# A first pass that puts four image rows on a partition and its filter taps on quarters of the array

## The chip, the core and the metric

The kernel runs on one core of one Trainium2 chip. The metric is the time of one execution in microseconds (us) of the device. Five engines work beside each other, each through its own list of instructions: TensorE (PE; its weight loads are a row of their own, PEld), VectorE (DVE), ScalarE (ACT), GpSimd (POOL) and SyncE (SP, which issues the transfers here). They meet at semaphores only. The transfers themselves are done by 16 DMA engines.

## The reference, cut to what matters

Two layers over x of shape 8 x 512 x 128 x 128, float32. The first layer halves the image by a grouped 3 x 3 convolution (two input channels make one of 256 output channels), finds clusters and a gate from that small image, and adds its gated, enlarged copy to x:

```
x1 = conv(x, w_down, strides (2, 2), padding 1, groups 256)     # 8 x 256 x 64 x 64
...                                                             # k-means, mixture, gate from x1
up = repeat(gate * x1 + x1, 2, axis=1) * w_up
x  = bilinear_up_x2(up) + x
```

The second layer projects that x on 8 x 8 cosine patterns over the image and uses the 64 numbers of each channel for an attention:

```
P  = einsum('hu,wv->hwuv', Dh, Dv)      # 16384 x 64
xP = einsum('bcn,nk->bck', x, P)
...                                     # attention from xP; gamma * out + x
```

Since the projection is linear, the kernel takes it of the raw x and of x1 apart.

## The kernel before, in words

The kernel has a first pass over all of x (268 MB), a short stretch that finds clusters and gates from what the pass left, and a second pass that reads x again and writes the output. The change is in `first_pass` and in the constants that it reads, and nowhere else.

**Tiles.** A unit is two input channels, that is one output channel, of all 8 images: 1 MB in `xt`, one of 14 buffers. A partition holds two adjacent rows (r = 0, 1) of one channel, so 2 channels x 64 pairs of rows fill the 128 partitions, and a piece of a load is 1 KB. Four units are a group; there are 64 groups.

**Tap products.** For each unit POOL builds `band`, three columns of 64 x 64 weights on 128 rows (lines 206 and 213). PE (`convolve`, line 278) makes the convolution of a pair of units in one PSUM bank: unit e = 0 on the left column half of the array and e = 1 on the right one, six taps each (two rows r, three column shifts dw), all 128 rows of the array. ACT copies the bank to `staged` (line 260), SP stores it to `xd` in DRAM (line 155) in pieces of 256 bytes, one row of 64 numbers of one image.

**Projection.** `project` (line 294) multiplies the group's x by the 8 cosines over the rows: 16 matmuls of 32 columns on four column quarters. DVE multiplies by the cosines over the columns and sums (lines 225 and 229). Every fourth group `project_low` (line 307) does the same with `staged`.

**What sets the order.** Each engine's list is written out. PE: the two pairs of a group, in every fourth group the small projection, then the group's projection. SP: the group's two stores (each waits for ACT's copy), then the loads of four units, which wait until the projection has freed their buffers; halfway and at the end eight stores of `freq` (`store_freq`, line 164). All transfers share SP's one queue and land in about the order of issue. POOL builds bands up to eight units ahead.

## Time and profile before

| | |
|---|---|
| median of 3 runs | 2952.55 us (2927.55 to 2962.68) |
| profiled execution | 2949.2 us, span 2947.4 us |
| first pass | to about 1007 us of the span |
| PE busy in the whole span | 2531.7 us (86%) |
| DVE, ACT, POOL busy | 2141.5, 1185.5, 1040.4 us |
| read and written in DRAM | 615.0 and 303.6 MB |

A row of the trace gives an engine, the line of the kernel that issued, the tiles (out<-in, buffer numbers left out) and times. Busy times of PE are unions of records whose ends are modelled, so the starts of its records tell more than their lengths. A matmul of the program leaves two records here. The share of the DMA engines is the sum of their packets' times over 16 engines, and can pass 1 where packets overlap. What an engine waited for is inferred from semaphores.

### The profile page before, as it was taken

How to read it: one execution, taken by the hardware profiler on the slowest of the kernel's cores; microseconds unless marked ns; L12 is line 12 of the kernel's file. 1: busy time of each engine (PE TensorE's matmuls, PEld its weight loads, DVE VectorE, ACT ScalarE, POOL GpSimd, SP SyncE). 2: the span in 40 equal slices, each digit the busy share in tenths (PEclk: the TensorE clock that was granted, in tenths of full speed). 3: DMA queues.
4: the chain of work that ended last, by engine and by line, in shares of the span. 5: the costliest groups of instructions: out<-in, count | busy, mean ns of one | idle time of the engine just before them, and what ended most of it. 6: DMA issues, size and time to landing. Idle time of an engine off the chain costs nothing.

```text
span 2947.4 us, 46132 instructions
## 1 busy us (share of the span) xinstructions
PE 2531.7 (86%) x17638; PEld 1666.6 (57%) x17638; DVE 2141.5 (73%) x2317; ACT 1185.5 (40%) x3193; POOL 1040.4 (35%) x772
## 2 busy tenths in 40 slices
PE   8999999999999666378499989888888887888887
PEld 2233223233323164044389888878778887788776
DVE  3777767677766743165499998988788888888886
ACT  0000000000000020033377777767666676766764
POOL 5444444444444000000044444444434343343433
PEclk9999999999999875689699999999999999999998
DMA  9999999999999660630499999999999999999998
GB/s 318 305 313 307 298 303 316 298 300 309 309 298 304 193 281 18 187 38 0 177 357 416 416 415 402 406 390 380 384 370 386 371 389 374 385 361 376 375 379 326
DMA packets 622924, 923.48 MB, mean 313 GB/s; under 512 B 208641, under 2 KB 471169, under 8 KB 620290
## 3 DMA queue, kind: packets, MB, share of 16 engines
q1 hardware_dynamic: 622722, 920.73, 90.1%
q8 instruction: 134, 2.20, 0.3%
q14 instruction: 68, 0.56, 0.0%
HBM read 615.00 MB, written 303.56 MB: 312 GB/s over the span
## 4 chain that ended last, share of the span: by engine, by line
DMA 33%; PE 11%; DVE 3%; ACT 2%; issue 2%; SPq 1%; POOL 0%; DVEq 0%
DMA out<-second_x 25%; PE second_o L1245 7%; DMA second_x<-in_x 4%; DMA second_dd<-downsampled 4%; DVE second_x L1469 1%; PE second_mid_t L1215 1%; DVE second_left L1018 1%; DVE second_mid L1450 1%; SPq L1051 1%; PE second_st L1105 1%; ACT second_mid L1334 1%; ACT second_left L1346 1%; POOL second_left L1018 0%; PE second_zt_t L1228 0%; ACT second_part L1334 0%
## 5 line engine op out<-in xcount | busy, mean ns | idle before, releaser
L1245 PE MATMUL second_o<-second_right,second_left 128*128 128x128 f32 x8192 | 1081.4, 281 | 110.9 <-issue 44.3
L1018 POOL TENSOR_TENSOR second_left<-second_mid_copy,second_coef_rep 64x1024 f32<-64x1024 f32 x256 | 608.6, 2377 | 1350.5 <-ACT second_mid_copy L1355 1329.5
L1245 PEld LDWEIGHTS second_o<-second_right,second_left 128*128 128x128 f32 x8192 | 999.3, 196 | 144.8 <-issue 134.7
L1469 DVE SCALAR_TENSOR_TENSOR second_x<-second_o,second_shift,second_x 128x512 f32<-128x512 f32 x1024 | 735.3, 738 | 222.9 <-PE second_o L1245 118.3
L278 PE MATMUL first_conv<-first_x,first_band 128*64 128x512 f32 (+1 forms) x3072 | 735.6, 618 | 19.4 <-POOL first_band L213 11.2
L278 PEld LDWEIGHTS first_conv<-first_x,first_band 128*64 128x64 f32 x3072 | 238.3, 135 | 510.5 <-issue 460.5
L225 DVE TENSOR_TENSOR first_product<-first_freq,first_cols 128x4096 f32<-128x4096 f32 x64 | 283.2, 4424 | 310.5 <-PE first_freq L294 310.0
L206 POOL TENSOR_TENSOR first_band<-first_shift,first_w_all 128x576 f32<-128x576 f32 x256 | 289.6, 1152 | 541.1 <-PE first_conv L278 533.8
L260 ACT ACTIVATE first_staged<-first_conv 128x512 f32<-128x512 f32 x128 | 76.5, 597 | 923.5 <-PE first_conv L278 923.5
L1334 ACT ACTIVATE second_mid<-second_dd,all_inter 128x128 f32<-128x128 f32 x1024 | 313.3, 388 | 85.8 <-DMA second_dd<-downsampled 83.6
L1334 ACT ACTIVATE second_part<-second_dd,all_inter 128x128 f32<-128x128 f32 x1024 | 313.2, 388 | 3.2
L1018 DVE TENSOR_TENSOR second_left<-second_mid_t,second_coef_rep 64x1024 f32<-64x1024 f32 x256 | 308.3, 1204 | 0.9 <-PE second_mid_t L1215 0.6
L229 DVE TENSOR_REDUCE first_freq<-first_product 128x32 f32<-128x4096 f32 x64 | 282.9, 4420 | 2.2
L1215 PE MATMUL second_mid_t<-all_const,second_mid 128*128 128x128 f32 x1024 | 166.3, 287 | 98.1 <-DVE second_mid L1450 97.4
L1355 ACT ACTIVATE second_mid_copy<-second_mid_t 64x512 f32<-64x512 f32 x256 | 151.6, 592 | 213.6 <-PE second_mid_t L1215 210.5
L294 PE MATMUL first_freq<-first_x,first_rows 128*32 128x512 f32 x2048 | 232.6, 594 | 0.0
L1215 PEld LDWEIGHTS second_mid_t<-all_const,second_mid 128*128 128x128 f32 x1024 | 118.2, 145 | 117.9 <-DVE second_mid L1450 113.9
L1450 DVE TENSOR_TENSOR second_mid<-second_mid,second_part 128x1024 f32<-128x1024 f32 x128 | 162.5, 1269 | 3.5 <-ACT second_part L1334 3.5
L294 PEld LDWEIGHTS first_freq<-first_x,first_rows 128*32 128x32 f32 x2048 | 61.5, 110 | 165.7 <-issue 165.7
L213 POOL TENSOR_TENSOR first_band<-first_band 128x192 f32<-128x192 f32 x256 | 147.4, 597 | 0.0
L1358 ACT ACTIVATE second_right<-second_zt_t 64x256 f32<-64x256 f32 x256 | 96.7, 378 | 122.0 <-PE second_zt_t L1228 120.5
L1228 PE MATMUL second_zt_t<-all_const,second_zt 128*128 128x128 f32 x512 | 101.8, 282 | 0.0
(219 smaller groups left out, 1415.9 us busy)
## 6 DMA issues: line engine op xcount, KB each, us to landing
first_x<-in_x SPq DMA_DIRECT2D x256, 1024.0 KB, 11.0
second_x<-in_x SPq DMA_DIRECT2D x256, 1024.0 KB, 14.3
out<-second_x SPq DMA_DIRECT2D x256, 1024.0 KB, 16.4
downsampled<-first_staged SPq DMA_DIRECT2D x128, 256.0 KB, 8.6
gather_d<-downsampled SPq DMA_DIRECT2D x16, 2048.0 KB, 16.4
second_dd<-downsampled SPq DMA_DIRECT2D x64, 512.0 KB, 14.9
second_p<-in_p_cols SPq DMA_DIRECT2D x1, 4096.0 KB
gates_ft<-all_wv SPq DMA_DIRECT2D x64, 32.0 KB, 5.4
```

The lines of the kernel that those rows point to most:

```text
L206: nc.gpsimd.tensor_tensor(band[unit % WEIGHTS1][:, :, :, :], shift[:, :, :].unsqueeze(2).broadcast_to([P, 3, 3, HD]), w_all[:, unit, :].re ...
L225: nc.vector.tensor_tensor(product[:, :, :, :], freq_ps[g % FREQ_BANKS][:, :, :].unsqueeze(2).broadcast_to(shape), cols[:, :, :].unsqueeze( ...
L229: nc.vector.tensor_reduce(freq[:, g, :, :], product[:, :, :, :], AX.X, ALU.add).then_inc(freq_summed, 1)
L278: last = nc.tensor.matmul(bank[e * HD:(e + 1) * HD, :, left:], band[unit % WEIGHTS1][:, 1 + r, dw + 1, :], xt[unit % SLOTS1][:, :, r, at:a ...
L294: last = nc.tensor.matmul(bank[32 * q:32 * q + 32, :, :], rows[:, r, j, :], xt[unit % SLOTS1][:, half * HALF_B:(half + 1) * HALF_B, r, :], ...
L1018: return eng.tensor_tensor(left[a][rows, odd:HALF:2, :, :].rearrange("p n (t s) g -> p n t s g", t=T), turned[rows, :, :, :].unsqueeze(3). ...
L1215: last = nc.tensor.transpose(mid_t[:, n, t, :], mid[m % 2][:, t, r:r + 2, :].rearrange("p h w -> p (h w)"), k("ident"))
L1245: last = nc.tensor.matmul(ob[n][:, r, :], left[a][:, r, n, :], right[a][:, r, :], start=True, stop=True)
L1334: last = nc.scalar.activation((mid[c], part)[r][:, :, 2 * i + 1 - e, :], dd[:, :, row(i + e + r - 1), :], ACT.Copy, scale=row_w[:, 2 * e + ...
L1355: nc.scalar.activation(mid_copy[hi, :, :, :], mid_t[hi, :, :, :], ACT.Copy).then_inc(mid_copied, 1)
L1450: nc.vector.tensor_tensor(mid[c][:, :, :, :], mid[c][:, :, :, :], part[:, :, :, :], ALU.add).then_inc(interpolated, 1)
L1469: nc.vector.scalar_tensor_tensor(out=xt[i][:, n // S, n % S, rows, :], in0=ob[n][:, :, :], scalar=shift[:, n:n + 1], in1=xt[i][:, n // S, ...
```

## The change

A tile is now four input channels (two output channels) with four adjacent rows of an image on a partition: 4 channels x 32 blocks of rows on the 128 partitions, 2 MB, loaded in pieces of 2 KB; seven buffers in place of fourteen, two tiles a group. A channel pair lies on one half of the partitions, so a tap product uses 64 rows of the array: k picks the row half (and the PSUM bank), a the tile and the column half. Rows r = 1 and r = 3 of a block serve an even and an odd output row each, so their products are 64 columns wide; r = 0 and r = 2 serve one, 32 wide. Even output rows stand on partitions 0 to 31 of a half, odd ones on 32 to 63; so a bank is stored by four transfers of 32 partitions in place of one. The bands come ready from one multiplication, as `shift` and the weights are laid out for it on the host.

```
-SLOTS1 = 14
-WEIGHTS1 = 8
+BLOCK1 = 4
+BLOCKS1 = H // BLOCK1
+TILES1 = GROUPS1 * 2
+SLOTS1 = 7
+WEIGHTS1 = 4
+EDGES = [(1, (2, 0)), (3, (0, 2)), (0, (1,)), (2, (1,))]
+BANDS = [dh for _r, dhs in EDGES for dh in dhs]
...
-    xv = x.rearrange("b (c s) (i r) w -> c (s i) b (r w)", s=S, r=2)
-    xdv = xd.rearrange("b t g (h w) -> (t g h) b w", w=WD)
+    xv = x.rearrange("b (n q) (i r) w -> n (q i) b (r w)", q=2 * S, r=BLOCK1)
+    xdv = xd.rearrange("b t g (i e w) -> (t g) e i b w", e=2, w=WD)
...
-        xt = [sc.sb(f"x{i}", [P, B, 2, W]) for i in range(SLOTS1)]
+        xt = [sc.sb(f"x{i}", [P, B, BLOCK1, W]) for i in range(SLOTS1)]
...
-                    if unit >= SLOTS1:
-                        sp.wait_ge(freq_made, (unit - SLOTS1) // GROUP1 + 1)
+                    if tile >= SLOTS1:
+                        sp.wait_ge(freq_made, (tile - SLOTS1) // 2 + 1)
...
                     sp.wait_ge(conv_copied, pair + 1)
-                    sp.dma_start(xdv[pair * P:(pair + 1) * P], staged[pair % STAGED][:, :, :]
-                                 ).then_inc(stored[pair % STAGED], 16)
+                    for a in range(2):
+                        for e in range(2):
+                            at = a * 64 + e * 32
+                            sp.dma_start(xdv[pair // 2 * GROUP1 + 2 * a + pair % 2, e], staged[pair % STAGED][at:at + 32, :, :]
+                                         ).then_inc(stored[pair % STAGED], 16)
...
                     for pair in (2 * g, 2 * g + 1):
                         store(pair)
-                    for unit in range(g * GROUP1 + SLOTS1, (g + 1) * GROUP1 + SLOTS1):
-                        if unit < UNITS1:
-                            load(unit)
+                    for tile in range(2 * g + SLOTS1, 2 * g + 2 + SLOTS1):
+                        if tile < TILES1:
+                            load(tile)
...
-                    for unit in units:
-                        b = band[unit % WEIGHTS1]
-                        pool.wait_ge(scaled, unit + 1)
-                        nc.gpsimd.tensor_tensor(b[:, 2, :, :], b[:, 2, :, :], b[:, 0, :, :], ALU.add).then_inc(banded, 1)
+                for tile in range(TILES1):
+                    if tile >= WEIGHTS1:
+                        pool.wait_ge(conv_made, (tile - WEIGHTS1) // 2 + 1)
+                    nc.gpsimd.tensor_tensor(
+                        band[tile % WEIGHTS1][:, :, :, :], shift[:, :, :].unsqueeze(1).broadcast_to(shape),
+                        w_all[:, tile, :].rearrange("p (a b) -> p a b", a=3).unsqueeze(3).broadcast_to(shape),
+                        ALU.mult).then_inc(banded, 1)
...
+                def convolve(g):
+
+                    if g >= CONV_BANKS // 2:
+                        pe.wait_ge(conv_copied, 2 * (g - CONV_BANKS // 2) + 2)
+                    pe.wait_ge(banded, 2 * g + 2)
+                    for tile in (2 * g, 2 * g + 1):
+                        pe.wait_ge(x_in[tile % SLOTS1], (tile // SLOTS1 + 1) * 16)
+
+                    def product(r, n, width, place, dw, first, last):
                         left = 1 if dw < 0 else 0
                         at = dw + 2 * left
+                        for a in range(2):
+                            for k in range(2):
+                                tile, part = 2 * g + a, slice(k * 64, k * 64 + 64)
+                                made = nc.tensor.matmul(
+                                    conv_ps[(2 * g + k) % CONV_BANKS][a * HD + place:a * HD + place + width * BLOCKS1,
+                                                                      :, left:],
+                                    band[tile % WEIGHTS1][part, dw + 1, n:n + width, :].rearrange("p n i -> p (n i)"),
+                                    xt[tile % SLOTS1][part, :, r, at:at + 2 * (WD - left) - 1:2],
+                                    start=first, stop=last)
+                        return made
+
+                    for dw in (0, 1, -1):
+                        product(1, 0, 2, 0, dw, dw == 0, False)
+                        product(3, 2, 2, 0, dw, False, False)
+                    for dw in (0, 1, -1):
+                        product(0, 4, 1, 0, dw, False, dw < 0)
+                        made = product(2, 5, 1, BLOCKS1, dw, False, dw < 0)
+                    made.then_inc(conv_made, 1)
...
-                    for n in range(4):
-                        j, r = n // 2, n % 2
+                    for r in range(BLOCK1):
                         for q in range(4):
-                            half, up = q // 2, q % 2
-                            unit = g * GROUP1 + 2 * up + j
-                            last = nc.tensor.matmul(bank[32 * q:32 * q + 32, :, :], rows[:, r, j, :],
-                                                    xt[unit % SLOTS1][:, half * HALF_B:(half + 1) * HALF_B, r, :],
-                                                    start=n == 0, stop=n == 3)
+                            half, a = q // 2, q % 2
+                            last = nc.tensor.matmul(
+                                bank[32 * q:32 * q + 32, :, :], rows[:, r, :],
+                                xt[(2 * g + a) % SLOTS1][:, half * HALF_B:(half + 1) * HALF_B, r, :],
+                                start=r == 0, stop=r == BLOCK1 - 1)
```

On SP, from the start of the program through the first groups, the list before was this (line, kind, out<-in, shape, how many in a row; L149 are the loads, L155 the stores):

```order
L174 DMA first_shift<-in_first_cols 128x192
L174 DMA first_rows<-in_first_cols 128x128
L174 DMA first_low_rows<-in_first_cols 128x64
L175 DMA first_w_all<-in_w_rows 128x2304
L149 DMA first_x<-in_x 128x8x256 x2
L180 DMA first_cols<-in_first_cols 128x1024
L180 DMA first_low_cols<-in_first_cols 128x512
L149 DMA first_x<-in_x 128x8x256 x12
L155 DMA downsampled<-first_staged 128x8x64 x2
L149 DMA first_x<-in_x 128x8x256 x4
L155 DMA downsampled<-first_staged 128x8x64 x2
L149 DMA first_x<-in_x 128x8x256 x4
```

With the change the same stretch has half as many loads of twice the size, and eight stores where two stood (L154 loads, L163 stores):

```order
L154 DMA first_x<-in_x 128x8x512 x2
L188 DMA first_cols<-in_first_cols 128x1024
L188 DMA first_low_cols<-in_first_cols 128x512
L154 DMA first_x<-in_x 128x8x512 x5
L163 DMA downsampled<-first_staged 32x8x64 x8
L154 DMA first_x<-in_x 128x8x512 x2
L163 DMA downsampled<-first_staged 32x8x64 x8
L154 DMA first_x<-in_x 128x8x512 x2
```

Stores still stand ahead of the loads of their group, in one block. On PE, the first group and the start of the second were this before (the shape is that of the result, columns of the array by elements):

```order
L278 MATMUL first_conv<-first_x,first_band 64x512 x8
L278 MATMUL first_conv<-first_x,first_band 64x8x63 x4
L278 MATMUL first_conv<-first_x,first_band 64x512 x8
L278 MATMUL first_conv<-first_x,first_band 64x8x63 x4
L294 MATMUL first_freq<-first_x,first_rows 32x512 x16
L278 MATMUL first_conv<-first_x,first_band 64x512 x8
```

And with the change (L282 the tap products, L306 the projection):

```order
L282 MATMUL first_conv<-first_x,first_band 64x512 x16
L282 MATMUL first_conv<-first_x,first_band 64x8x63 x8
L282 MATMUL first_conv<-first_x,first_band 32x512 x16
L282 MATMUL first_conv<-first_x,first_band 32x8x63 x8
L306 MATMUL first_freq<-first_x,first_rows 32x512 x16
L282 MATMUL first_conv<-first_x,first_band 64x512 x16
```

There are 48 tap products a group where 24 stood, 24 of them 64 columns wide and 24 of them 32, each on 64 rows of the array; the projection keeps its 16.

## Rows read from the trace of the kernel before

**Rows 1.** Busy by stretch, first pass: PE, PEld, DVE, ACT, POOL, PEclk, DMA share, GB/s
```profile
0.00:1007.00 1007.00, 987.18 (x5376) 306.61 (x5376) 691.89 (x157) 77.76 (x129) 431.76 (x516) 1.00 1.01 303
```

**Rows 2.** Costliest groups on the page, PE and POOL of the first pass
```profile
L278 PE MATMUL first_conv<-first_x,first_band 128*64 128x512 f32 (+1 forms) x3072 | 735.6, 618 | 19.4 <-POOL first_band L213 11.2
...
L206 POOL TENSOR_TENSOR first_band<-first_shift,first_w_all 128x576 f32<-128x576 f32 x256 | 289.6, 1152 | 541.1 <-PE first_conv L278 533.8
...
L294 PE MATMUL first_freq<-first_x,first_rows 128*32 128x512 f32 x2048 | 232.6, 594 | 0.0
...
L213 POOL TENSOR_TENSOR first_band<-first_band 128x192 f32<-128x192 f32 x256 | 147.4, 597 | 0.0
```

**Rows 3.** PE in order of time, 88 to 165 us: start, length, line
```profile
101.84 3.64 PE L294 MATMUL first_freq<-first_x,first_rows 128*32 128x512 f32 x32
105.41 11.03 PE L278 MATMUL first_conv<-first_x,first_band 128*64 128x512 f32 x48
116.37 3.64 PE L294 MATMUL first_freq<-first_x,first_rows 128*32 128x512 f32 x32
...
130.89 3.64 PE L294 MATMUL first_freq<-first_x,first_rows 128*32 128x512 f32 x32
...
147.16 3.62 PE L294 MATMUL first_freq<-first_x,first_rows 128*32 128x512 f32 x32
```

**Rows 4.** Weight loads in order of time, 405 to 413 us
```profile
407.03 0.14 PEld L278 LDWEIGHTS first_conv<-first_x,first_band 128*64 128x64 f32 x2 [0.31 <-issue]
407.48 0.14 PEld L278 LDWEIGHTS first_conv<-first_x,first_band 128*64 128x64 f32 x2 [0.30 <-issue]
...
409.81 0.13 PEld L294 LDWEIGHTS first_freq<-first_x,first_rows 128*32 128x32 f32 x4 [0.30 <-issue]
410.24 0.13 PEld L294 LDWEIGHTS first_freq<-first_x,first_rows 128*32 128x32 f32 x4 [0.30 <-issue]
```

**Rows 5.** Waits to 1100 us, PE's for loads: us in total, times, longest
```profile
PEld first_conv L278 <- DMA first_x<-in_x: 26.8, 30, 2.8
...
PE first_conv L278 <- DMA first_x<-in_x: 8.0, 10, 1.8
```

**Rows 6.** Waits of SP's queue, to 1007 us
```profile
SPq L155 <- ACT first_staged L260: 70.8, 50, 4.2
SPq L149 <- PE first_freq L294: 67.3, 51, 3.1
```

**Rows 7.** Line 294 alone: durations, first and last start
```profile
L294 PE MATMUL first_freq<-first_x,first_rows x2048: 592/592/617, 27.5 to 1004.3; 128*32 128x512 f32 x187
```

**Rows 8.** SP in order of time, 300 to 350 us: start, length, line
```profile
306.12 5.81 SPq L155 DMA_DIRECT2D downsampled<-first_staged  x2
311.97 9.64 SPq L149 DMA_DIRECT2D first_x<-in_x  x4
321.65 6.25 SPq L155 DMA_DIRECT2D downsampled<-first_staged  x2
```

**Rows 9.** Busy by stretch, as rows 1: store stretch, next loads, second pass
```profile
312.00:318.00 6.00, 6.00 (x42) 1.48 (x38) 0.00 (x0) 0.60 (x1) 3.36 (x4) 1.00 0.82 202
318.00:327.00 9.00, 8.81 (x40) 2.66 (x38) 8.81 (x2) 0.60 (x1) 3.27 (x4) 1.00 1.09 353
...
1600.00:1700.00 100.00, 92.55 (x763) 85.50 (x761) 92.00 (x121) 76.78 (x215) 44.62 (x19) 1.00 1.03 416
```

**Rows 10.** DMA packets, stretches 16–44 (loads), 1425.5–1428 (2 KB loads), 996.5–999 us (stores)
```profile
DMA packets 9654, 9.75 MB, mean 348 GB/s; under 512 B 144, under 2 KB 9653, under 8 KB 9653
...
DMA packets 520, 1.00 MB, mean 400 GB/s; under 512 B 32, under 2 KB 32, under 8 KB 520
...
DMA packets 2181, 0.55 MB, mean 220 GB/s; under 512 B 2181, under 2 KB 2181, under 8 KB 2181
```

**Rows 11.** Issues: loads on the page, to landing; SP in time, 1010–1020 us
```profile
first_x<-in_x SPq DMA_DIRECT2D x256, 1024.0 KB, 11.0
...
1013.89 4.13 SPq L164 DMA_DIRECT2D projected<-first_freq  x8
```

More of the change, by code:

```diff
@@ L175, in _ @@
                 sp.dma_start(w_all[:, :, :].rearrange("p c k -> p (c k)"), w_rows).then_inc(const_in, 16)
-                for unit in range(SLOTS1):
-                    load(unit)
-                    if unit == 1:
+                for tile in range(SLOTS1):
+                    load(tile)
+                    if tile == 1:
                         for n in (3, 4):
@@ L184, in _ @@
                         store(pair)
-                    for unit in range(g * GROUP1 + SLOTS1, (g + 1) * GROUP1 + SLOTS1):
-                        if unit < UNITS1:
-                            load(unit)
+                    for tile in range(2 * g + SLOTS1, 2 * g + 2 + SLOTS1):
+                        if tile < TILES1:
+                            load(tile)
                     if g == GROUPS1 // 2:
@@ L193, in _ @@
                 for i in range(STAGED):
-                    sp.wait_ge(stored[i], len(range(i, pairs, STAGED)) * 16)
+                    sp.wait_ge(stored[i], len(range(i, pairs, STAGED)) * 64)
                 sp.wait_ge(freq_out, 2 * 2 * GROUP1 * 16)
@@ L272, in convolve @@
                         left = 1 if dw < 0 else 0
                         at = dw + 2 * left
-                        for e in range(2):
-                            unit = 2 * pair + e
-                            if n == 0:
-                                pe.wait_ge(x_in[unit % SLOTS1], (unit // SLOTS1 + 1) * 16)
-                            last = nc.tensor.matmul(bank[e * HD:(e + 1) * HD, :, left:],
-                                                    band[unit % WEIGHTS1][:, 1 + r, dw + 1, :],
-                                                    xt[unit % SLOTS1][:, :, r, at:at + 2 * (WD - left) - 1:2],
-                                                    start=n == 0, stop=n == len(TAPS) - 1)
@@ L282, in convolve @@
-                    last.then_inc(conv_made, 1)
+                        for a in range(2):
[7 more added lines that the diff above has]
+                                    start=first, stop=last)
@@ L1598, in shape_constants @@
     side, high, low = row // UV, row // LOW % LOW, row % LOW
-    own, at = row // HD, row % HD
-    halo = np.stack([at[:, None] + 1 == np.arange(HD)[None, :]] + [at[:, None] == np.arange(HD)[None, :]] * 2, 1)
-    turned = np.stack([[d[2 * at + r][:, None, :] * (2 * j + own[:, None, None] == np.arange(4)[None, :, None])
-                        for j in range(2)] for r in range(2)]).transpose(2, 0, 1, 3, 4)
-    low_turned = np.stack([du[at][:, None, :] * (2 * j + own[:, None, None] == np.arange(4)[None, :, None])
+    own, at = row // BLOCKS1, row % BLOCKS1
+    here_, next_ = at[:, None] == np.arange(BLOCKS1)[None, :], at[:, None] + 1 == np.arange(BLOCKS1)[None, :]
+    halo = np.stack([next_ if n == 2 else here_ for n in range(len(BANDS))], 1)
+    turned = np.stack([d[BLOCK1 * at + r][:, None, :] * (own[:, None, None] == np.arange(4)[None, :, None])
+                       for r in range(BLOCK1)], 1)
+    half, h_low = row // HD, 2 * (row % BLOCKS1) + row // BLOCKS1 % 2
+    low_turned = np.stack([du[h_low][:, None, :] * (j + 2 * half[:, None, None] == np.arange(4)[None, :, None])
                            for j in range(2)], 1)
```

46 lines of the change are left out of this document (16 added, 30 removed).

## The prediction

> **What bounds the kernel now.** I first read the busy table by stretch [rows 1]: the first pass, to 1007 us, keeps PE busy 987 us of 1007 and the DMA engines at 1.01, while DVE has 692, POOL 432 and ACT 78. The change touches this stretch alone, so two candidates are left. The costliest groups [rows 2] say what PE does in it: 3072 records of L278 (the tap products), 2048 of L294 (the projection), two records for each matmul of the program. A busy PE is no proof of a bound, so the second view is the order of time on PE where nothing waits [rows 3]. From one projection to the next it is 14.53 us (101.84 to 116.37), and 16.27 us in every fourth group, which has L307 too (130.89 to 147.16). Over four groups that is 59.86 us, 14.97 each: the pace PE would keep if never held. The weight loads give the step [rows 4]: tap products start every 0.45 us, two records at a time (column halves); projections every 0.43 us, four at a time (column quarters). So 24 steps of 0.45 = 10.80 of the 10.96 us from 105.41 to 116.37, and 8 of 0.43 = 3.44 of the 3.57 us after it; 0.16 and 0.13 us go at the changes of tile shape.
>
> The real pace is slower. L294 starts from 27.5 to 1004.3 us [rows 7]; less the last projection's seven steps that is 63 groups in 973.8 us, 15.46 each. The 0.49 us between this and 14.97, times 64, is 31 us, and the waits list has it: 26.8 + 8.0 us for first_x [rows 5]. SP waits 71 + 67 us in all [rows 6], and over whole groups it sits inside one issue after the other [rows 8]. **PE and DMA are both near their limit, DMA slightly nearer.** A gain needs both.
>
> What DMA does with a group of 4.19 MB of loads and 0.52 MB of stores is in the stretches. Loads alone, 1 KB packets, run at 348 GB/s [rows 10], so they take 12.05 us. The stores' stretch (312 to 318 us) moves only 202 GB/s at a share of 0.82, and the next is back at 353 [rows 9]. In those 6 us 1.21 MB moved, 0.69 MB of it loads, worth 1.97 us at 350; the group's stores took the other 4.03 us. Stores alone run at 220 GB/s [rows 10], 2.38 us a group. The rest is lost in the turn from stores to loads. On the mean over the pass, 15.46 − 12.05 = 3.41 us is what a group's stores cost.
>
> **The change, part by part.**
>
> *Loads.* 256 loads of 1 MB in 1 KB pieces become 128 of 2 MB in 2 KB pieces, the same bytes. The trace has 2 KB loads by themselves for 2.5 us: 400 GB/s [rows 10]. So 10.49 us a group, 1.56 less. The bounds are 348 (no gain) and the 416 GB/s of 4 KB packets later in the run [rows 9]; I take 400, the same packet size, though from a short stretch.
>
> *Stores.* The same 256-byte pieces, but eight issues of 64 KB a group in place of two of 256 KB. The nearest rows are the eight 64 KB stores of L164, taken up in 4.13 us, 0.52 each [rows 11]. SP then needs 8 × 0.52 + 2 × 0.5 = 5.2 us a group, well inside 14. The turn to loads stays once a group, since the eight follow each other. I keep 3.41 us; ends 2.38 (turn hidden) and 4.03. The new stride in DRAM (every second row) I cost at nothing, as each piece was separate already; the upper end holds it otherwise.
>
> *Tap products.* Per group 48 matmuls in place of 24, each on half the rows. The 64-wide ones (24, rows r = 1 and 3) fill four quarters of the array, the 32-wide ones (24, r = 0 and 2) come as two products on different column quarters, so eight fit. If what fits runs together, that is 12 + 6 = 18 steps of 0.45 where 24 stood, 2.70 us less, and one more change of shape, 0.15 more: 14.53 becomes 11.98, the mean over four 12.4. No row shows row halves, so I bound it: steps as short as now, or one half after the other. I take the first because the projection's four streams [rows 4] show the array taking unlike operands at once without a longer step; eight records per step at the spacing of those is still no burden.
>
> *POOL.* 256 second steps (L213, 147 us) and one of two waits go; 128 builds of 576 elements stay at 1.15 us [rows 2]. POOL was hidden behind PE, so nothing is gained: its 2.3 us a group are covered by the two groups that it builds ahead. DVE's order is unchanged, 692 / 64 = 10.8 us a group, under any period here. ACT's two copies (78 / 128 = 0.6 us each) now follow each other; ACT has little else to do.
>
> *Lead and ends.* Seven 2 MB buffers hold what fourteen did. After project(g) SP loads the second tile of group g+3 and the first of g+4, and PE needs g+3 two groups later, 28 us, against 11.0 to land now [rows 11]. PE's start now wants 4 MB in place of 2, some 6 us later, which a pass bound by loads doesn't feel.
>
> **The sum.** A group is 10.49 + 3.41 = 13.90 us, above PE's 12.4. The last load follows the stores of 61 groups: 64 × 10.49 + 61 × 3.41 = 879 us, behind some 6 us of constants (2.2 MB by their shapes, at 350), so 885. Then PE does the last taps and seven steps of projection, 8.4 + 3.0: its last start is at 896 against 1004.3, **108 us earlier**. All behind it is unchanged work on unchanged data. Against the profiled execution (2949.2 us, span 2947.4; the median of the runs is 2952.6, 0.1% above) that gives 2841; I add 6 us for PE holding the queue in some groups, its 12.4 being near: **2847 us**. With stores at 2.38 it would be about 2780, at 4.03 some 2880; loads at 380 instead of 400 add 35.
>
> **A rule against it.** The eight 64 KB stores in [rows 11] were taken up every 0.52 us. The Trainium skill's page "DMA: Bandwidth & Descriptors", section Bandwidth, calls small transfers descriptor-dominated and gives 0.95 us for a load of 64 KB issued from GpSimd; by an estimate from it eight would take 7.6 us, the group 18.1 and the run about 3120. The trace does not agree: 0.52 us is a little over half of that.
>
> **Rivals.**
>
> *Loads no faster.* If HBM or the writing beside it, and not the packets, holds loads near 350, the group stays at 12.05 + 3.41 and the time at 2940 to 2950; in between, 2895 to 2940. For it: in [rows 10] the 2 KB stretch is short and has no stores beside it. Against: 348, 400, 416 rise with the packet. Chance 0.08.
>
> *Small products four at a time.* If the two 32-wide products don't share the array, 24 steps stay, PE's floor is 14.97 + 0.15, times 64 = 968 us, and with the later start and a few waits the pass ends where it did: 2940 to 2960. Against: the 32-wide projections run four at once. Chance 0.08. The Trainium skill's page "TensorEngine Tiling (Array Packing)", section Tiling Modes, lists 64×64 as four independent tiles and 64×32 as eight; no row here can show it.
>
> *Row halves one after the other (slower).* Where matmuls on different row halves are not overlapped, the taps take 24 + 12 steps, 16.2 us in place of 10.8. The group is 14.97 + 5.4 + 0.15 = 20.5, the pass 1313 us and some 20 of start: about 330 us later, 3280. It decides as soon as a group's taps need more than 25 steps. Chance 0.06.
>
> *Each store issue pays the turn (slower).* The 3.41 − 2.38 = 1.03 us lost per group may belong to an issue's completion, 0.51 each, and not to the turn to loads. Eight then cost 2.38 + 4.1 = 6.5, the group 17.0, the run 2949 + 64 × 1.5 = 3045. It decides from 0.32 us an issue, (15.46 − 10.49 − 2.38) / 8. For it: the stretch at 202 GB/s [rows 9] has two issues and no other cause shown. Against: in the stretch of stores alone [rows 10] issue follows issue at 220 GB/s. Chance 0.04.
>
> **Chances and range.** The forecast, 2780 to 2895, has 0.74. What this kernel's runs can tell from no change is about 2%, 59 us, so below 2893: faster 0.74, same 0.16 (the first two rivals), slower 0.10. The range 2785 to 2915 holds nearly all of the forecast and the nearer half of the first rival.
>
> **What the new profile would show.** Loads alone near 400 GB/s and PE's steps still 0.45 us with four, then eight, records starting together; a projection every 13.9 us, and PE waiting for first_x by about 1.5 us a group. Starts of the 64-wide products every 0.9 us would prove the third rival, six more steps in the 32-wide part the second, a GB/s row still near 350 the first. If the stretches with stores run longer than now, it is the fourth. I am wrong altogether if the first pass ends after 970 us.

## The result: 2993.4 us, slower by 1.5%

The changed kernel takes 2993.4 us (2979.2 to 3003.0), the kernel before 2948.6 beside it: a ratio of 1.0154, 95% interval 1.0079 to 1.0229. That lies within the 2% that the forecast called no change, though the interval is clear of 1. The forecast was 2847 us, the range 2785 to 2915. The profiled execution took 2993.5 us, its span 2991.7.

The first pass by stretch, columns as in [rows 1], the second row the first loads with hardly a store beside them:

```profile
0.00:1050.00 1050.00, 859.67 (x8448) 267.93 (x8448) 695.15 (x158) 70.76 (x129) 145.69 (x132) 0.93 0.93 291
16.00:44.00 28.00, 24.67 (x244) 7.47 (x248) 8.85 (x2) 2.17 (x4) 4.20 (x4) 1.00 1.05 389
```

PE's work fell from 987 us [rows 1] to 860, POOL's from 432 to 146, and loads by themselves rose from 348 GB/s [rows 10] to 389. Yet DMA moves 291 GB/s over the pass, where it moved 303. The projection's line in the changed kernel shows what that costs:

```profile
L306 PE MATMUL first_freq<-first_x,first_rows x2048: 592/592/617, 29.8 to 1044.0; 128*32 128x512 f32 x187
```

The last projection starts 39.7 us later than in [rows 7]. By the count used for the forecast a group now takes (1044.0 − 29.8 − 3.0) / 63 = 16.05 us, where it took 15.46. PE did its share. Its weight loads in order of time:

```profile
127.12 0.18 PEld L282 LDWEIGHTS first_conv<-first_x,first_band 64*64 64x64 f32 x4 [0.27 <-issue]
127.57 0.18 PEld L282 LDWEIGHTS first_conv<-first_x,first_band 64*64 64x64 f32 x4 [0.27 <-issue]
...
132.69 0.17 PEld L282 LDWEIGHTS first_conv<-first_x,first_band 64*32 64x32 f32 x8 [0.28 <-issue]
```

Four products of 64 columns, or eight of 32, start together every 0.45 us, row halves included. On PE in order of time, a group's taps then take 8.54 us, and the projection follows; the rest is waiting for loads:

```profile
110.93 10.87 PE L282 MATMUL first_conv<-first_x,first_band 64*64 64x512 f32 x96 [5.04 <-DMA first_x<-in_x]
...
126.19 8.54 PE L282 MATMUL first_conv<-first_x,first_band 64*64 64x512 f32 x96 [0.82 <-DMA first_x<-in_x]
134.66 3.64 PE L306 MATMUL first_freq<-first_x,first_rows 128*32 128x512 f32 x32
141.25 8.54 PE L282 MATMUL first_conv<-first_x,first_band 64*64 64x512 f32 x96 [2.95 <-DMA first_x<-in_x]
```

Over the pass PE waits 186.5 us for first_x, where [rows 5] had 34.8 us in all. The longest wait, 19.3 us, is for the first tiles; the rest is 2.7 us in each later group:

```profile
PE first_conv L282 <- DMA first_x<-in_x: 186.5, 56, 19.3
```

What the DMA engines do meanwhile stands in 40 slices of 1 us, 300 to 340 us, GB/s in each:

```profile
GB/s 389 393 347 303 133 68 81 103 66 129 303 393 410 408 399 387 389 389 387 360 318 159 124 75 68 94 274 371 412 408 399 387 385 387 391 373 338 209 95 81
```

A group is some eleven slices at 300 to 412 and five or six at 66 to 160: its stores, and the loads' slow return. The DMA engines are not full in these, with a share of 0.46 at 322 to 324 us and 0.62 at 324 to 326. By subtraction, as for the forecast: a group's 4.194 MB of loads at 389 GB/s are 10.78 us, and **its stores cost 16.05 − 10.78 = 5.27 us**, where 3.41 was kept. (The expectations below count loads in pieces per us, which gives up to 0.2 us more or less.)

### The profile page after: what moved, and what is told of

Read it like the earlier page. It is cut to its first block, busy times and chain, and to the rows that moved or that the text cites. A ratio compares the mean times of both kernels' runs of the same rounds, so it can differ in the third digit from the quotient of the medians.

```text
span 2991.7 us, 52146 instructions
## 1 busy us (share of the span) xinstructions
PE 2407.1 (80%) x20710; PEld 1627.9 (54%) x20710; DVE 2140.9 (72%) x2317; ACT 1178.3 (39%) x3193; POOL 754.3 (25%) x388
## 4 chain that ended last, share of the span: by engine, by line
DMA 34%; PE 8%; DVE 3%; ACT 3%; issue 1%; SPq 1%; POOL 0%; DVEq 0%; ACTq 0%
DMA out<-second_x 27%; PE second_o L1257 5%; DMA second_dd<-downsampled 4%; DMA second_x<-in_x 3%; DVE second_x L1481 1%; DVE second_left L1030 1%; ACT second_left L1358 1%; PE second_st L1117 1%; SPq L1063 1%; PE second_mid_t L1227 1%; ACT second_mid L1346 1%; DVE second_mid L1462 1%; ACT second_part L1346 1%; PE second_zt_t L1240 0%; POOL second_left L1030 0%
## 5 line engine op out<-in xcount | busy, mean ns | idle before, releaser
L282 PE MATMUL first_conv<-first_x,first_band 64*64 64x512 f32 (+2 forms) x6144 | 604.0, 655 | 186.7 <-DMA first_x<-in_x 186.5
L282 PEld LDWEIGHTS first_conv<-first_x,first_band 64*64 64x64 f32 (+1 forms) x6144 | 199.7, 127 | 587.1 <-issue 587.1
L263 ACT ACTIVATE first_staged<-first_conv 128x512 f32<-128x512 f32 x128 | 69.5, 595 | 970.8 <-PE first_conv L282 970.8
L213 POOL TENSOR_TENSOR first_band<-first_shift,first_w_all 128x576 f32<-128x576 f32 x128 | 145.5, 1158 | 865.9 <-PE first_conv L282 858.9
L306 PE MATMUL first_freq<-first_x,first_rows 128*32 128x512 f32 x2048 | 232.6, 594 | 0.0
L306 PEld LDWEIGHTS first_freq<-first_x,first_rows 128*32 128x32 f32 x2048 | 61.5, 110 | 167.0 <-issue 166.1
L1370 ACT ACTIVATE second_right<-second_zt_t 64x256 f32<-64x256 f32 x256 | 96.5, 377 | 122.3 <-PE second_zt_t L1240 120.8
L1371 ACT ACTIVATE second_right<-second_zt_t 64x256 f32<-64x256 f32 x256 | 96.9, 378 | 2.9
```

What stands on the lines that cost most here:

```text
L213: nc.gpsimd.tensor_tensor(band[tile % WEIGHTS1][:, :, :, :], shift[:, :, :].unsqueeze(1).broadcast_to(shape), w_all[:, tile, :].rearrange( ...
L282: made = nc.tensor.matmul(conv_ps[(2 * g + k) % CONV_BANKS][a * HD + place:a * HD + place + width * BLOCKS1, :, left:], band[tile % WEIGHT ...
L306: last = nc.tensor.matmul(bank[32 * q:32 * q + 32, :, :], rows[:, r, :], xt[(2 * g + a) % SLOTS1][:, half * HALF_B:(half + 1) * HALF_B, r, :],
```

## Why SP is no help: how its rows are read

SP in order of time, changed kernel:

```profile
322.17 1.24 SPq L154 DMA_DIRECT2D first_x<-in_x  x2
323.46 15.17 SPq L163 DMA_DIRECT2D downsampled<-first_staged  x8
```

Its waits, to 1050 us, blame ACT for part of this, and hardly ever a buffer that is not free yet:

```profile
SPq L163 <- ACT first_staged L263: 233.7, 55, 6.2
...
SPq L154 <- PE first_freq L306: 0.2, 1, 0.2
```

The first row misleads. The eight stores that start at 323.46 are the 145th to 152nd, group 18 counted from 0. Its copies are ACT's 37th and 38th:

```profile
309.75 1.08 ACT L263 ACTIVATE first_staged<-first_conv 128x512 f32<-128x512 f32 x2 [16.25 <-PE first_conv L282]
```

They were done at 310.83, 12.6 us before. SP is held in the issues themselves: eight take 15.2 us here, 4.1 where nothing holds them (stores_last, below). I read this as a queue that takes new work only as old work leaves; the trace doesn't show what the queue holds. So SP runs far behind PE: the loads issued from 322.17 us bring the slices back up from 326, some 4 us later, and the buffers for seven tiles give no lead.

## Experiments

Group times are the mean over the first pass, worked out as above; unless said otherwise, kernels are edits of the changed one. In the code "..." marks a cut; counts of semaphores that follow from the number of issues are left out. Where an expectation says that rows stand in another order or place, what is computed from them is other than the reference's, while the first pass keeps its instructions and bytes.

### Number, shape and stride of the stores

**one_store**: one issue per pair, to adjacent rows.

```diff
-                    for a in range(2):
-                        for e in range(2):
...
+                    sp.dma_start(xdv[pair * P:(pair + 1) * P], staged[pair % STAGED][:, :, :]
+                                 ).then_inc(stored[pair % STAGED], 16)
```

> The changed kernel with one store of 128 partitions to adjacent rows per pair, as the kernel before has it; the small image lands in DRAM with rows and channels in another order than the reference wants, the rest is as in the change. The changed kernel took 2993 us with a group of its first pass every 15.9 us, 10.8 of them loads at 389 GB/s. Theory issue (each store issue pays a turn), theory stride (every second row in DRAM is slower to write) and theory narrow (a store from 32 partitions is slower) all expect a group of 13.9 us and 2850 to 2870 us. Theory turn (the loss after a group's stores is longer with 2 KB loads behind them, whatever the stores are) expects 15.5 us and 2960 to 2995.

**four_contiguous**: four issues of 32 partitions, to adjacent rows.

```diff
+                    for n in range(4):
+                        sp.dma_start(xdv[pair * P + 32 * n:pair * P + 32 * n + 32], staged[pair % STAGED][32 * n:32 * n + 32, :, :]
...
```

> The changed kernel with four stores of 32 partitions per pair, each to 32 adjacent rows (again in another order than the reference wants). Issue: 2980 to 3000 us, a group of 15.9. Narrow: the same. Stride: 2850 to 2870. Turn: 2960 to 2995.

**one_strided**: one issue per pair, to every second row.

```diff
+    xdv = xd.rearrange("b t g (j e w) -> e (t g j) b w", e=2, w=WD)
...
+                    sp.dma_start(xdv[pair % 2, pair // 2 * P:(pair // 2 + 1) * P], staged[pair % STAGED][:, :, :]
```

> The changed kernel with one store of 128 partitions per pair to every second row in DRAM (again in another order than the reference wants). Stride: 2980 to 3000 us. Issue and narrow: 2850 to 2870. Turn: 2960 to 2995.

Measured: one_store 2969.6 us (ratio 1.0059, 1.0030 to 1.0087), group 15.65; four_contiguous 2989.9 us (1.0161, 1.0125 to 1.0197), group 15.98; one_strided 2963.4 us (1.0065, 1.0045 to 1.0085), group 15.65. The stride costs nothing (15.65 with it and without). Eight issues of 32 partitions in place of two of 128 cost 0.33 us a group to adjacent rows and 0.40 as the change has them, 25 us of the run; whether their number or their 32 partitions costs it, no run tells apart. Two stores of 256 KB as before still cost 15.65 − 10.78 = 4.87 us: most of the loss lies elsewhere.

**before_split**: the same question to the kernel before, its two stores as eight issues.

```diff
-                    sp.dma_start(xdv[pair * P:(pair + 1) * P], staged[pair % STAGED][:, :, :]
-                                 ).then_inc(stored[pair % STAGED], 16)
+                    for at in range(0, P, 32):
+                        sp.dma_start(xdv[pair * P + at:pair * P + at + 32], staged[pair % STAGED][at:at + 32, :, :]
+                                     ).then_inc(stored[pair % STAGED], 16)
```

> The kernel before with one edit: every store of 128 partitions issued as four of 32 partitions to the same addresses (eight store issues in a group in place of two). Theory (in the changed kernel the four issues cost about 0.35 to 0.4 us a group, and the rest has another cause): the same here, group 15.8 us, 2970 to 2975 us. Rival (the issue of 64 KB each 0.5 us holds back the loads behind it, wherever it stands): eight issues instead of two cost 1.9 us a group, group 17.3 us, about 3067 us.

Measured: 2972.5 us (1.0062, 1.0018 to 1.0107), group 15.80, so 0.34 us for six issues more. The price is about the same in both kernels.

### Taking the stores out of the loads' queue

**stores_on_act**: ScalarE issues each store behind its copy, on its own queue.

```diff
-                    for pair in (2 * g, 2 * g + 1):
-                        store(pair)
...
+                    act.wait_ge(conv_copied, pair + 1)
+                    for a in range(2):
+                        for e in range(2):
+                            at = a * 64 + e * 32
+                            act.dma_start(xdv[pair // 2 * GROUP1 + 2 * a + pair % 2, e], staged[pair % STAGED][at:at + 32, :, :]
+                                          ).then_inc(stored[pair % STAGED], 16)
```

> The changed kernel, all computed, with the stores of the small image issued by ACT behind its copies, on ACT's own queue. In the runs so far a group's stores cost 3.6 us of DMA time before the change and 5.0 to 5.4 after it, 2.4 of it the stores themselves and the rest lost while the engines come back from stores to loads. Theory turn (the loss belongs to the change from stores to loads in one queue): with two queues an engine has loads to do all the time, a group takes 13.1 to 13.9 us, the run 2815 to 2860. Theory write (256-byte pieces keep DRAM busy for 5 us a group, whatever stands beside them): a group of 15.5 to 16, the run 2960 to 2995.

Measured: **2758.9 us (0.9367, 0.9328 to 0.9406), faster than both kernels** and than either theory had it, group 12.47:

```profile
L301 PE MATMUL first_freq<-first_x,first_rows x2048: 592/592/617, 31.5 to 820.4; 128*32 128x512 f32 x187
```

Its GB/s in the same 40 slices, and its first pass by stretch:

```profile
GB/s 387 394 390 392 396 386 391 391 386 406 375 377 395 385 389 394 388 392 392 383 393 408 364 385 388 391 391 389 395 396 380 396 385 373 397 392 389 393 379 400
```
```profile
0.00:823.00 823.00, 801.66 (x8448) 234.73 (x8448) 691.88 (x157) 77.75 (x129) 145.69 (x132) 1.00 1.05 372
```

The same issues with the same bytes, and no gap: loads and stores run side by side, by the trace's packets (2 KB of a load, 256 bytes of a store) some 350 GB/s of loads and 40 of stores in each slice. PE, busy for 802 of 823 us, is the bound; it waits for loads once, 20.2 us at the start. SP now waits for something real:

```profile
SPq L154 <- PE first_freq L301: 245.0, 58, 9.2
```

In the Trainium skill, "DMA: Bandwidth & Descriptors" says under "Issuing engines are not separate DMA queues" that a second issuing engine saves only the time of issuing; here the second queue gave 3.6 us a group. SP's own time for issuing is not what was saved: stores_spread, below, keeps all eight issues on SP and takes 14.10 us. The section "Queues, rings and completion order" of the same page has each DMA engine turn round-robin between the queues that have work, and with that the slices agree.

**stores_last**: all 512 stores behind the last load. ACT's copies no longer wait for them, so the stores find only the last copies in the twelve buffers, and the small image is filled with these.

```diff
-                    for pair in (2 * g, 2 * g + 1):
-                        store(pair)
...
+                for pair in range(pairs):
+                    store(pair)
...
```

> The changed kernel with no store of the small image among the loads; all 512 follow at the end of the first pass, with what the 12 buffers then hold, so the small image in DRAM is wrong. Every theory: PE's own pace comes out, a group of 12.4 us, the last projection at about 820 us, load time 10.8 us a group under it; then some 150 us of stores at 220 GB/s, the run 2915 to 2940. If a group stays above 13 us, something other than the stores holds the loads.

Measured: 3015.9 us in a single run, where 2915 to 2940 was expected. Without stores between the loads a group takes 12.46 us, PE's pace again. The stores then stand alone:

```profile
800.00:1100.00 300.00, 21.54 (x236) 6.02 (x228) 42.00 (x11) 2.17 (x4) 0.00 (x0) 0.54 0.58 131
```

SP issued them in 260 us, not 150: 0.51 for each issue of 64 KB. From 830 to 1070 us, where they stand alone, that is 129 GB/s at a DMA share of 0.61. Stores that stand by themselves in 64 KB issues are slow, and that time is there to be shared with loads.

**turns_of_four**: the stores of four groups together, so a quarter of the turns.

```diff
+                    if g % 4 == 3:
+                        for pair in range(2 * g - 6, 2 * g + 2):
+                            store(pair)
...
```

> The changed kernel, all computed, with the stores of four groups issued together in every fourth group, one queue as before. Turn: the loss comes once in four groups, 2.4 + 3.0 / 4 = 3.2 us a group, a group of 13.9, the run 2850 to 2870. Write: the loss grows with the bytes stored and stays 5.2 us a group: 2980 to 2995.

Measured: 2951.7 us (1.0022, 0.9996 to 1.0049), group 15.58. Fewer turns help by 0.47 us a group, no more, which lies between the two theories. 32 issues in a row run at 0.51 us each, 4.1 us a group with hardly a load beside them; that is most of the 15.58 − 10.78 = 4.80 us which the stores still cost.

**before_act**: the kernel before with its two stores a group on ScalarE's queue.

```diff
+                    act.wait_ge(conv_copied, pair + 1)
+                    act.dma_start(xdv[pair * P:(pair + 1) * P], staged[pair % STAGED][:, :, :]
+                                  ).then_inc(stored[pair % STAGED], 16)
...
```

> The kernel before with one edit: ScalarE issues the two stores of a group on its own queue, SP only the loads. Theory (loads and stores that share SP's one queue don't run beside each other): the kernel before loses by it too, and its groups fall from the mean of 15.46 us to TensorE's own pace of about 14.97 us, 63 x 0.5 = 31 us less: about 2918 us. Rival (the kernel before was bound by TensorE's 14.97 us and the clock in the first place, and 0.5 us a group is start and end): no difference, 2945 to 2950 us. Rival (a second queue costs the loads of 1 KB pieces their rate): slower.

Measured: 2915.8 us (0.9863, 0.9825 to 0.9901), group 14.94: PE's 14.97 of [rows 3]. The kernel before had the gap too, but PE could give back only half a microsecond. Its slices still fall to 38 GB/s in places: SP now waits 418.7 us in all for buffers that PE has to free, and such a gap costs nothing.

### The order on one queue

**one_store_spread** and **stores_spread** have the order store, load, store, load, the first with one issue per pair, the second with the change's four; **before_spread** has store, two loads, store, two loads in the kernel before.

```diff
-                    for pair in (2 * g, 2 * g + 1):
-                        store(pair)
-                    for tile in range(2 * g + SLOTS1, 2 * g + 2 + SLOTS1):
-                        if tile < TILES1:
-                            load(tile)
+                    for n in range(2):
+                        store(2 * g + n)
+                        if 2 * g + n + SLOTS1 < TILES1:
+                            load(2 * g + n + SLOTS1)
```

> The changed kernel with one store for a pair to adjacent rows (the order of the rows in the small image is another), and on SP store, load, store, load in a group, where it was store, store, load, load (that kernel's group took 15.65 us, 2969.6 us). Theory (what is lost is the gap that a run of stores makes in the loads, and a load that stands between two stores fills it in part): the stores cost 3.6 us a group as in the kernel before, where the two stores of a group stand half a group apart: group 14.1 to 14.3 us, 2870 to 2885 us. Rival (every store stops the loads for the same time, whether they stand together or not): group 15.6 to 15.7 us, 2965 to 2972 us.

> The changed kernel with one edit: on SP the four stores of a pair, a load, the four stores of the other pair, a load, where it was eight stores and two loads. Theory (the loss is the gap that 512 KB of stores in a row make in the loads; 256 KB in a row leave a load in the queue beside them): the group falls from 16.05 us to that of the kernel with one store for a pair in this order, 13.55 us, and 0.3 to 0.5 us for the six further issues, 13.9 to 14.1 us: 2855 to 2870 us. Rival (eight issues of 64 KB keep SP so long that the loads stop in any order): above 2930 us.

> The kernel before with one edit: on SP a store, two loads, a store, two loads, where it was two stores and four loads. Theory (the gap of 512 KB of stores in a row is what costs, in this kernel too): the loads go on beside the stores, and TensorE's own pace is left, 14.99 us a group as with the stores on ScalarE's queue (2915.75 us): 2912 to 2922 us. Rival (2 MB in four loads of 1 KB pieces are 2048 pieces between the stores, and the queue holds little more, so that each store still stops the loads): 2940 to 2960 us.

Measured: one_store_spread 2832.8 us (0.9597, 0.9560 to 0.9635), group 13.55, better than either theory said (its expectation has the two stores of the kernel before half a group apart; by [rows 8] SP issues them in a row); stores_spread 2868.7 us (0.9720, 0.9649 to 0.9792), group 14.10; before_spread 2917.3 us (0.9854, 0.9803 to 0.9905), group 14.94, PE's pace. The projection's line and the slices of stores_spread:

```profile
L305 PE MATMUL first_freq<-first_x,first_rows x2048: 592/592/617, 31.0 to 922.6; 128*32 128x512 f32 x187
GB/s 333 319 243 273 337 266 246 305 378 334 245 226 302 322 340 342 374 315 323 371 350 358 402 357 307 325 369 352 348 381 330 279 321 327 334 279 365 382 283 306
```

Nothing falls under 226. By the packets, as a mean over the runs of stores from 100 to 760 us (a run ends where no store packet starts for 2 us), loads move 235 GB/s between the first and the last packet of a run of 256 KB here, and 80 beside a run of 512 KB in the changed kernel. I take this for a load that is still in the queue beside 256 KB of stores; the queue itself isn't in the trace. ScalarE, too, issues its stores four at a time, so of the 3.58 us that stores_on_act gains, the order alone can give 1.95, and the second queue the other 1.63. This edit changes the order of the issues and no byte, and turns the change from 1.5% slower into 2.8% faster.

### Why two stores in a row cost more than before

one_store and the kernel before issue the same two stores in a row, at 4.87 and 3.41 us. Pieces and addresses of the loads differ.

**loads_1k** and **one_store_loads_1k**: each load as two of 1 MB in 1 KB pieces, with the change's eight stores and with two. The second has number, size and pieces of the kernel before; a load takes every second 1 KB of four channels, where it took all of two.

```diff
+                    for h in range(2):
+                        sp.dma_start(xt[slot][:, :, 2 * h:2 * h + 2, :].rearrange("p b r w -> p b (r w)"),
+                                     xv[tile][:, :, h * 2 * W:(h + 1) * 2 * W]).then_inc(x_in[slot], 16)
...
```

> The changed kernel with each 2 MB load issued as two of 1 MB, two rows each, so in 1 KB pieces. Turn, with a loss that grows with the size of the load's pieces: loads at 350 GB/s take 12.0 us a group, the stores 3.5 to 3.9 as before the change: 15.5 to 16, the run 2955 to 2985. If the larger loss comes from anything else in the change (row halves of PE, the store issues), it stays 5.4: 17.4 us a group, 3070.

> The changed kernel with one store for a pair to adjacent rows (the order of the rows in the small image is another) and each load as two of 1 MB in 1 KB pieces: the DMA issues of a group are then, in number, size and piece, those of the kernel before (two stores of 256 KB, four loads of 1 MB), only that both stores of a group come at its end. Theory (what the stores cost depends on the number of issues and on where they stand): loads 11.98 us a group at 342 pieces a us, stores 5.0 us as with 2 KB pieces: group 17.0 us, 3050 to 3058 us. Rival (the queue's depth counts in pieces, and with 1 KB pieces and two stores all is as in the kernel before): stores 3.5 us, group 15.5 us, 2955 to 2962 us.

Measured: loads_1k 3076.2 us (1.0436, 1.0385 to 1.0487), group 17.45; one_store_loads_1k 3064.8 us (1.0370, 1.0334 to 1.0406), group 17.17, 1.7 more than the kernel before for the same list of issues. Going back to 1 KB pieces does not bring the old price back: at the 346 GB/s of its first loads (16 to 44 us) a group's loads take 12.12 us, which leaves 5.05 for the two stores.

**before_four_channels** gives the kernel before these addresses, **one_store_two_channels** gives one_store_loads_1k those of the kernel before.

```diff
 # before_four_channels
-    xv = x.rearrange("b (c s) (i r) w -> c (s i) b (r w)", s=S, r=2)
+    xv = x.rearrange("b (n q) (i r) w -> n (q i) b (r w)", q=2 * S, r=4)
...
+                                 xv[unit // 2][:, :, unit % 2 * 2 * W:(unit % 2 + 1) * 2 * W]
 # one_store_two_channels
-    xv = x.rearrange("b (n q) (i r) w -> n (q i) b (r w)", q=2 * S, r=BLOCK1)
+    xv = x.rearrange("b (c s) (i r) w -> c (s i) b (r w)", s=S, r=2)
...
```

> The kernel before with one edit: a load reads the addresses that half a tile of the changed kernel would, every second 1 KB piece of four channels, where it was all 1 KB pieces of two channels (the rows then stand in other places, and what is computed from them is not the reference's); number, size and pieces of the issues, the order and the buffers stay. Theory (the addresses of a load set how slowly the loads come back after the stores, and make the stores 1.6 us dearer): group 15.46 + 1.7 = 17.1 us, 3050 to 3060 us. Rival (the addresses do nothing): 2940 to 2960 us.

> The changed kernel with one store for a pair and each load as two of 1 MB in 1 KB pieces, as before (group 17.2 us, 3064.8 us), and the addresses of these loads those of the kernel before: all pieces of two channels each (the rows then stand in other places, and what is computed from them and the order of the small image are not the reference's). Theory (addresses): the stores cost 3.5 us again, group 15.5 us, 2955 to 2965 us. Rival (the addresses do nothing, something in the timing of TensorE does): 3055 to 3070 us.

Measured: before_four_channels 3070.9 us (1.0374, 1.0318 to 1.0429), group 17.45; one_store_two_channels 2963.7 us (1.0023, 0.9999 to 1.0047), group 15.65. **With 1 KB pieces, addresses alone cost 2.0 us a group put on one side and give back 1.5 taken off the other.** The projection's line of before_four_channels, and the same 40 slices of the kernel before and, second, of before_four_channels:

```profile
L295 PE MATMUL first_freq<-first_x,first_rows x2048: 592/592/617, 28.9 to 1131.4; 128*32 128x512 f32 x187
```

```profile
GB/s 105 250 317 379 370 357 354 349 349 348 354 349 331 297 145 85 119 233 332 381 376 350 349 346 348 348 349 342 338 283 143 94 84 294 340 343 377 383 351 350
```
```profile
GB/s 79 167 118 243 278 341 385 374 346 284 213 294 380 367 316 286 149 124 88 176 198 217 308 365 387 358 343 246 309 381 382 341 316 245 80 19 76 216 201 269
```

The peak is the same; what differs is the slow return behind the stores, and dips within the loads. Why the memory answers so is not shown.

The packets have a slow return with 2 KB pieces as well. In the first, second and third us behind a run of stores (means over the runs from 100 to 760 us) loads move 159, 322 and 346 GB/s in the kernel before, and 72, 151 and 300 in one_store; it is 69, 157 and 193 in before_four_channels, and 167, 314 and 341 in one_store_two_channels. The run of stores itself lasts 3.66 us in the kernel before and 4.23 in one_store.

**one_store_halves** and **spread_halves** were to give the 2 KB pieces two channels a load, by loading the halves of the partitions apart, the first with one issue per pair and the second with the order of stores_spread.

```diff
+                    for k in range(0, P, 64):
+                        sp.dma_start(xt[slot][k:k + 64, :, :, :].rearrange("p b r w -> p b (r w)"),
+                                     xv[tile][k:k + 64]).then_inc(x_in[slot], 16)
...
```

> The changed kernel with one store for a pair to adjacent rows (the order of the rows in the small image is another; group 15.65 us, 2969.6 us), and each load of 2 MB as two of 1 MB, the two halves of the partitions: two whole channels each, still in 2 KB pieces. Theory (a load over four channels comes back slowly after the stores, whatever its pieces): the stores cost 3.5 us as in the kernel before, group 14.0 to 14.2 us, 2865 to 2880 us. Rival (the addresses mattered only because every second 1 KB was left out, not for 2 KB pieces): group 15.6 to 15.9 us, 2965 to 2985 us. Rival (64 partitions a load use fewer of the DMA engines): slower than 2990 us.

> The changed kernel with the order four stores, a load, four stores, a load on SP (group 14.15 us, 2868.7 us), and each load as two of 1 MB, one for each half of the partitions (two whole channels each). Theory: with both causes gone TensorE's pace of about 12.5 us is nearly reached, group 12.5 to 13.2 us, 2760 to 2805 us. Rival (in this order the addresses no longer matter, because loads and stores run side by side): 2860 to 2880 us.

Measured: 3387.6 us (1.1495, 1.1444 to 1.1545) and 3299.3 us (1.1180, 1.1132 to 1.1228). The stretch of the first loads in one_store_halves says why:

```profile
16.00:44.00 28.00, 14.91 (x128) 4.39 (x128) 0.98 (x1) 1.09 (x2) 2.28 (x2) 1.00 1.07 224
```

The rival on half the partitions held in its time, but not in its reason of fewer engines: the mean DMA share is 1.07, at 224 GB/s (214 from 30 to 44 us, when the constants are in). The question they were made for stays open.

## Why the prediction was wrong

**The step that failed** is the one on the stores, "The turn to loads stays once a group, since the eight follow each other. I keep 3.41 us". That cost is 5.27 us, above the end of 4.03. Of the 1.86 us, 0.40 is the six further issues, or their 32 partitions (one_store; before_split has 0.34). The remaining 1.46 is what one_store costs beyond the kernel before: the run of stores is longer, and the loads come back more slowly behind it. With 1 KB pieces the loads' addresses make a difference of 1.5 to 2.0, and I take it for the same cause, but no run shows it for 2 KB pieces, so the cause of these 1.46 us stays open. Nor is the cost a turn in the main: a run of stores lasts 3.66 us before the change and 4.52 after it, with loads at 68 and 80 GB/s beside it. And the low end of 2.38 took the 220 GB/s of 256 KB issues; the 64 KB issues of the change ran at 129 GB/s by themselves (stores_last). Where the stores stand decides what of it is paid: the order alone brings 5.27 to 14.10 − 10.78 = 3.32 us, and with the second queue at most 12.47 − 10.78 = 1.69 is left, behind PE's own pace. A mean cost was carried from one kernel to the other without asking what it was made of.

Point by point:

- *Loads*: 400 GB/s forecast, 389 measured, 10.78 us in place of 10.49. Right but for 0.29. Together with the stores' 1.86 that is 2.15 us a group, 138 of the 148 us by which the last projection is late (1044 against 896).
- *Tap products*: 18 steps of 0.45 us and a group of 11.98, measured 126.19 to 134.66 and on to the projection's end at 138.30, 12.1 us; the mean over four, 12.4 forecast, is 12.46 in stores_last. Right, and worth nothing while the loads set the pace.
- *SP*: "5.2 us a group, well inside 14" was wrong. Issues of 64 KB do take 0.5 us where nothing holds them, but here SP is held for 15.2 us by eight and for 1.2 by the loads, the whole group. [rows 8] showed it before: from 306.12 to 321.65 us, one issue after the other, is 15.5, a full group. The prediction saw SP "inside one issue after the other" and drew nothing from it for the sum.
- *Lead*: seven buffers, 28 us, never came into play, since the queue and not the buffers decides when a load goes out. Landing took 15.0 us, not 11.0.
- *POOL and stride*: both free, as said.
- *Rivals*: the sign was the fourth's, longer stretches of stores, but not its price: an issue costs 0.40 / 6 = 0.07 us beside the loads, not 0.51, and its 17.0 us a group was not reached. Longer stretches of stores were a poor sign for it, as the same two issues gave them in one_store. The first three are refuted by the rows above. That the same stores get dearer behind other loads was among no rival.

## What to carry to other kernels

Where loads and stores share a queue, read the GB/s in slices of 1 us and ask how many bytes of stores stand in a row: a gap in the slices can be time that another order, or another engine's queue, gives back before any engine is made faster, unless the loads wait there for buffers, as in before_act. When a load's layout changes, its rate alone is not its price: here the addresses also set how fast 1 KB loads came back after writes. And compare the time of a store's issue with the end of the work it stores, before a wait in the list is believed.

## Not expected of the hardware

- Loads onto 64 partitions moved 214 GB/s (30 to 44 us) with the DMA share at 1.07, onto 128 partitions 389. "DMA: Bandwidth & Descriptors" of the Trainium skill, section "Rules for kernel authors", says that transfers to the two halves serialize and advises against them; here they cost more than that.
- Loads that read every second 1 KB of four channels lose under 2% of the rate where hardly a store stands beside them (342 against 348 GB/s, and 346 against 352, at 16 to 44 us), but 1.5 to 2.0 us a group with stores, against loads that read two whole channels.
- After a wait of 5.04 us PE took 10.87 us for taps that otherwise took 8.54. A later group shows the granted clock: PE has no work from 313.21 to 316.57 us, runs at the lower level of 1.2 GHz (0.50) in 318 to 320, and is at 2.4 GHz (1.00) again from 322; its taps take 10.14 us. It sets nothing here, since PE waits for loads again before the next taps. Two stretches, columns as in [rows 1]:

```profile
314.00:316.00 2.00, 0.00 (x0) 0.00 (x0) 2.00 (x1) 0.00 (x0) 0.00 (x0) 1.00 1.05 393
...
318.00:320.00 2.00, 2.00 (x12) 0.64 (x8) 2.00 (x1) 0.00 (x0) 0.00 (x0) 0.50 1.06 374
```
